# Down product waiting tile by tile, input placed in three steps, late queries inside the last unit

## The reference

```
h = layernorm(x) * w + b
win = windows of 14 x 14 of h, padded (four per image, most of them part full)
q, k, v = split(win @ qkv_w + qkv_b)                 # 12 heads of 16
a = softmax(q * scale @ k.T + rel_h(q) + rel_w(q))   # relative position terms, made from q
x1 = x + unwindow(a @ v) @ proj_w + proj_b
x  = x1 + gelu(layernorm(x1) @ up_w + up_b) @ down_w + down_b     # hidden width 768
```

## Time and profile before

| | |
|---|---|
| median of 3 runs | 676.68 us (676.61 to 677.33) |
| the profiled execution's own time | 682.86 us |
| its span, first to last instruction | 681.1 us |
| TensorE busy | 623.2 us, 92% |
| VectorE, ScalarE busy | 53%, 49% |
| GpSimd busy | 19% |

### The profile page before, as it was taken

The page is one execution under the profiler, slowest core; times in us unless marked ns, Lnnn a source line. Parts: engine busy times, 40 slices in busy tenths (PEclk is TensorE's granted clock), DMA queues, the critical chain, the costliest instruction groups (busy, mean ns, idle before and its releaser), DMA issues.

```text
span 681.1 us, 14753 instructions
## 1 busy us (share of the span) xinstructions
PE 623.2 (92%) x5696; PEld 480.5 (71%) x5696; DVE 360.6 (53%) x989; ACT 334.0 (49%) x807; POOL 129.9 (19%) x172
## 2 busy tenths in 40 slices
PE   3799999999999999999999999999999999899996
PEld 2587776777677768775877587758775876477674
DVE  4447463746374637462655365546552764426665
ACT  3326743674367435744474447543744365315453
POOL 1800032003300330023002400140013000412220
PEclk9959999999999999999999999999999999799998
DMA  4774670067205720571047003700280000000000
GB/s 110 163 154 119 135 168 7 3 133 153 69 2 124 160 59 3 113 157 36 3 87 162 22 2 77 172 22 2 66 184 21 3 3 1 1 24 1 24 24 23
DMA packets 33175, 47.51 MB, mean 70 GB/s; under 512 B 5563, under 2 KB 14331, under 8 KB 33107
## 3 DMA queue, kind: packets, MB, share of 16 engines
q1 hardware_dynamic: 31874, 46.18, 29.5%
q10 hardware_dynamic: 1232, 0.40, 0.2%
HBM read 7.25 MB, written 1.57 MB: 13 GB/s over the span
## 4 chain that ended last, share of the span: by engine, by line
issue 55%; PE 25%; POOL 12%; DVE 4%; ACT 2%; DMA 1%; POOLq 0%; ACTq 0%; SPq 0%; DVEq 0%
POOL xn L821 4%; POOL q_nat L802 3%; PE bank L631 2%; PE bank L580 2%; PE bank L625 2%; PE bank L497 2%; PE bank L516 2%; PE bank L390 2%; PE bank L431 2%; POOL x_all L808 2%; POOL x_all L814 2%; POOL rstd L795 1%; PE bank L467 1%; PE bank L614 1%; PE bank L598 1%
## 5 line engine op out<-in xcount | busy, mean ns | idle before, releaser
L1268 ACT ACTIVATE PT<-bank 98x392 f32<-98x392 f32 (+1 forms) x288 | 136.8, 490 | 134.1 <-PE bank L497 130.0
L983 DVE TENSOR_REDUCE neg_max<-bank 98x2 f32<-98x392 f32 x192 | 106.4, 562 | 116.6 <-PE bank L467 116.1
L497 PE MATMUL bank<-q_aug,k_aug 127*98 127x196 f32 (+1 forms) x672 | 112.9, 264 | 0.9 <-ACT PT L1268 0.3
L467 PE MATMUL bank<-k_aug,q_aug 126*98 126x196 f32 x384 | 87.4, 314 | 11.2 <-DVE neg_max L983 9.6
L497 PEld LDWEIGHTS bank<-q_aug,k_aug 127*98 127x98 f32 (+1 forms) x672 | 88.0, 168 | 10.5 <-ACT PT L1268 5.8
L802 POOL TENSOR_TENSOR q_nat<-st_q 96x392 f32<-96x392 f32 (+2 forms) x48 | 24.9, 546 | 330.9 <-DVE st_q L951 330.9
L580 PE MATMUL bank<-w_down,PT 128*128 128x192 f32 x384 | 74.1, 330 | 7.0 <-ACT PT L1299 7.0
L467 PEld LDWEIGHTS bank<-k_aug,q_aug 126*98 126x98 f32 x384 | 56.1, 169 | 33.7 <-DVE neg_max L983 15.9
L390 PE MATMUL bank<-xT,w_qkv 97*96 97x256 f32 (+2 forms) x272 | 75.5, 393 | 1.8 <-ACT xT L1205 1.4
L580 PEld LDWEIGHTS bank<-w_down,PT 128*128 128x128 f32 x384 | 61.8, 190 | 8.7 <-ACT PT L1299 8.2
L981 DVE TENSOR_REDUCE neg_max<-bank 120x1 f32<-120x318 f32 x96 | 46.5, 485 | 33.5 <-PE bank L463 33.4
(11 more groups left out here) (97 smaller groups left out, 968.0 us busy)
## 6 DMA issues: line engine op xcount, KB each, us to landing
q_aug<-st_q SPq DMA_DIRECT2D x64, 192.0 KB
k_aug<-st_k SPq DMA_DIRECT2D x64, 192.0 KB, 5.0
q_aug<-st_r SPq DMA_DIRECT2D x64, 168.0 KB
x_all<-in_x SPq DMA_DIRECT2D x4, 384.0 KB, 5.9
q_aug<-negT ACTq DMA_DIRECT2D x96, 1.5 KB
k_aug<-st_p SPq DMA_DIRECT2D x16, 74.2 KB, 2.3
w_up<-in_w_up SPq DMA_DIRECT2D x2, 576.0 KB, 5.0
w_down<-in_down_w SPq DMA_DIRECT2D x4, 288.0 KB, 5.6
```

Source lines behind the costliest of these rows:

```text
L467: last = t_.matmul(b[0:HALF, WIN * r:WIN * r + WIN], q_aug[0:NEG, h, c + HALF * r:c + HALF * r + HALF], k_aug[0:NEG, h, c:c + WIN], start= ...
L497: last = t_.matmul(b[0:keys, m * k:m * k + m], k_aug[0:NEG + 1, h, c + keys * k:c + keys * k + keys], q_aug[0:NEG + 1, h, c:c + m], start= ...
L983: ins = v.tensor_reduce(neg_max[0:HALF, slot(n, u), e:e + 5:4], b[0:HALF, 0:2 * WIN] .rearrange("p (r m) -> p r m", r=2), AX.X, ALU.max, n ...
L1268: s.activation(PT[0:rows, i % 8, 0:m], bank[2 + i % 2][0:rows, 0:m], ACT.Exp).then_inc(S["exp"], 1)
```

## The change

Three edits. In `down` the single wait for all six GELUs at t = 0, f = 0 becomes four: three GELUs at f = 0 (the third reads bank 2, which the product of t = 0 writes), four at f = 3, five at f = 4, six at f = 5; the early scores between the matmuls move from behind f = 1 and f = 4 to behind f = 3 and f = 5. `place_x` on VectorE is called three times, behind the row maxima of steps 1, 2 and 3 of unit 0, one piece each, and its semaphore rises three times a job. The four chunks of the late queries stand behind the four steps of unit 8.

```
-                   xT_dve=1, xT_act=1, q_mm=2, ...
+                   xT_dve=3, xT_act=1, q_mm=2, ...
...
-                    need(pe, ["xT_dve", "xT_act"][j], m, 1)
+                    need(pe, ["xT_dve", "xT_act"][j], m, [3, 1][j])
...
-                        need(pe, "xT_dve", n, 1)
+                        need(pe, "xT_dve", n, 3)
                         need(pe, "xT_act", n, 1)
...
             def down(n, t, f):
                 l = layer(n)
-                if t == 0 and f == 0:
-                    need(pe, "gelu", n, MC)
+                if t == 0 and f != 1 and f != 2:
+                    need(pe, "gelu", n, max(3, f + 1))
                 if t == 2 and f == 0:
                     need(pe, "out", n, 1)
...
-                            if u == 8 and e in (0, 3):
-                                queries_in(n + 1, 1, e // 3, 1)
+                            if u == 8:
+                                queries_in(n + 1, 1, e, 1)
...
-                if more:
-                    queries_in(n + 1, 1, 2, 2)
                 for k in range(3):
                     values(n, LAST, k)
...
                         down(n, t, f)
-                        if more and f in (1, 4):
+                        if more and f in (3, 5):
                             early_scores(n + 1, 4 + 2 * t + f // 4)
...
-            def place_x(n):
+            def place_x(n, k):
                 l = layer(n)
-                need(dve, "xT_mm", n, 1)
-                need(dve, "v_mm", n - 1, 3)
-                dve.wait_ge(ld_front[l], LD_FRONT)
-                for dst, src in pieces(xT[0:96, 0, 0:TOK], bank[front_bank(n, "x0")][0:96, :]):
-                    last = v.tensor_scalar(dst, src, affine[l][0:96, 0, 0:1], affine[l][0:96, 1, 0:1], ALU.mult, ALU.add)
-                last.then_inc(S["xT_dve"], 1)
+                if k == 0:
+                    need(dve, "xT_mm", n, 1)
+                    need(dve, "v_mm", n - 1, 3)
+                    dve.wait_ge(ld_front[l], LD_FRONT)
+                dst, src = pieces(xT[0:96, 0, 0:TOK], bank[front_bank(n, "x0")][0:96, :])[k]
+                v.tensor_scalar(dst, src, affine[l][0:96, 0, 0:1], affine[l][0:96, 1, 0:1], ALU.mult, ALU.add)\
+                    .then_inc(S["xT_dve"], 1)
...
-            place_x(0)
+            for k in range(3):
+                place_x(0, k)
...
                         if more:
-                            if (u, e) == (0, 1):
-                                place_x(n + 1)
+                            if u == 0 and e:
+                                place_x(n + 1, e - 1)
```

More of the change, by code:

```diff
@@ L192, in program @@
         PER = dict(stats1=1, stats2=2, aggr1=1, aggr2=2, veps1=1, veps2=2, rstd1=1, rstd2=2, xn1=1, xn2=2, xT_mm=2,
-                   xT_dve=1, xT_act=1, q_mm=2, q_hi=2, q_lo=2, q_nat=2, k_mm=2, k_hi=2, k_lo=2, r_tok=4, rt_copy=4, r_mm=4, r_hi=4, r_lo=4,
+                   xT_dve=3, xT_act=1, q_mm=2, q_hi=2, q_lo=2, q_nat=2, k_mm=2, k_hi=2, k_lo=2, r_tok=4, rt_copy=4, r_mm=4, r_hi=4, r_lo=4,
                    v_mm=3, v_copy=3, s_mm=HEADS, max=HEADS, nt_mm=UNITS, negT=UNITS, st_mm=HEADS, exp=HEADS,
```

## The result

The changed kernel takes 672.3 us in the median of 17 runs, the kernel before 676.8 us on the same chip. The ratio is 0.9932, 95% interval 0.9906 to 0.9958: faster by 4.5 us, or 0.7%. The forecast was 671.2 us with a range of 668.5 to 674.3.

The account below looks back on a forecast made before the run. TensorE, busy 92% of the span, was taken as the bound, so only closing its idle time pays. Terms -8.3 + 0.3 + 0.6 + 1.9 = -5.5 us took the median from 676.7 to 671.2 us, range 668.5 to 674.3.

Parts of the forecast that it names:

- down product: Down matmuls no longer wait for GELUs 5 and 6: 1.19 us saved, seven times, 8.3 us.
- last job's wait: In the last job, TensorE's 0.88 us wait around VectorE's clearing of the fold tiles grows by 0.3 us, once.
- placing: Wait before score 16 is split, not closed; first query projection still needs piece three: +0.08 us, seven times, +0.6 us.
- late queries: Last unit: two chunks moved before score 35 delay the last value product 0.27 us, seven times, +1.9 us.
- refill: TensorE array emptied at each added down wait: taken as nothing, upper bound 0.1 us each, 2.1 us in all.
- alternation on VectorE: Pieces and row maxima taking turns: might lose four overlaps, projection 0.28 us later, +2.0 us over seven jobs.
- upper end: Placing term's upper bound, +2.6 us, if VectorE instructions lose their overlap, as the skill's DRAIN rule would have it.
- (a): Rival: spread placing removes the whole 1.13 us VectorE wait before score 16; 662.7 us, chance 0.08.
- (b): Rival: late queries in the last unit cost nothing, their shift staying under 0.48 us; 669.3 us, chance 0.12.
- (c): Rival: refill at down waits or VectorE overlap lost, 2.0 to 2.1 us each; 673.3, both 675.3 us; chance 0.10.
- (d): Rival: all upper ends together, -0.1 us, no change that can be told; chance 0.04.
- (e): Rival: DMA of negated maxima into q_aug holds the next job's first transposed score, gain lost; 679.5 us, chance 0.04.

Follow-up runs that it names:

- e7: Late queries edit alone on the kernel before, with ScalarE's output copy of unit 7 put ahead of the last exponential: +0.08 us a job, one run.
- e8: Kernel before with only late query chunk 1 moved, behind step 1 of unit 8: -0.02 us a job, one run.
- e3: Late queries edit alone on the kernel before: +0.40 us a job, ratio 1.0036.
- e2: Placing in three steps alone on the kernel before: +0.10 us a job, ratio 0.9989.
- e13: Kernel before plus down edit, VectorE's pieces all in unit 1, ScalarE's in unit 0, early query chunks all in unit 2: -1.31 us a job, ratio 0.9820.
- e1: Down product's waits and moved early scores alone on the kernel before: -1.21 us a job, ratio 0.9883.
- e12: Kernel before plus down edit, VectorE's pieces two and three in unit 1, ScalarE's three in unit 0, early query chunks later: -1.49 us a job, ratio 0.9833.
- e9: Kernel before plus down edit, pieces two and three of both VectorE and ScalarE in unit 1, early query chunks later: -0.72 us a job, ratio 0.9890.
- e11: Kernel before plus down edit, all three pieces of both engines in unit 1, early query chunks in unit 2: -0.81 us a job, ratio 0.9908.

## Why the prediction was right

The time came out 1.1 us above the forecast and within its own narrower range; the terms, by one-part kernels, seven jobs each, and the last job's by its score 14:

| term | taken | measured |
|---|---|---|
| down product | -8.3 | -1.21 x 7 = -8.5 |
| last job's wait | +0.3 | +0.3 |
| placing | +0.6 | +0.10 x 7 = +0.7 |
| late queries | +1.9 | +0.40 x 7 = +2.8 |
| sum | -5.5 | -4.7 |

**Down product: right.** No refill and no gap at any of the added waits, and 1.19 us forecast against 1.21. The Trainium skill ("TensorE: Matmul & The Clock Gate", Step-by-step: what each phase is for) has weight loads pulled ahead of matmuls in flight, and leaves open whether that lasts across a wait. This trace shows that it does where the semaphore is already there: the eight instructions take the 1.18 us from 104.64 to score 4 at 105.82, and the weight load of f = 3, which waits for the fourth GELU, starts at 105.47, while the matmul in front of it (105.47 to 105.79) is at work.

**The last job: right in size, a little off in form.** The wait of 0.88 us didn't grow (0.87 after); a wait of 0.19 us for an earlier row maximum stands in front of it, and score 14 comes 0.3 us later than a job's gain alone would put it.

**Placing: right.** The wait was split, not closed: score 16 sooner by 0.50 us, the projection later by 0.06, when 0.08 had been taken. The alternation on VectorE kept its overlap: the piece that ends at 117.07 is followed at 117.00. The Trainium skill ("VectorE: DVE Perf Modes", The DRAIN you can't avoid) lets the next instruction wait for an empty pipe, but adds that one that isn't held starts earlier, which the prediction left out. The rows of both orders fit the addition, with an overlap of 0.07 us, so the section was no reason for the upper end. The forecast looked for the remainder as waits of L390 and L497. None is listed for these jobs: 0.13 us is idle before the projection, and transposed score 4 starts 0.48 us behind its score with the idle time hidden in the modelled end of the score.

**Late queries: the mechanism right, the size off.** This is the term that was mis-sized: +1.9 us taken, 2.8 measured. e7 and e8 confirm the mechanism (the cover of ScalarE's exponential and copy, a threshold above one chunk). The step that failed in size was "value product at 152.01 with the 0.05 us from an end on ScalarE to a start on TensorE", 0.27 us later. It came 0.40 later. Of the 0.13 missing, 0.09 is that last distance, 0.14 us where the copy comes last; the rest is the shift of ScalarE's last exponential, 0.77 to 0.79 us in e3 instead of 0.75. The 0.05 us was read at a down matmul that waits for one semaphore, and it holds for this product too when the exponential is last (e7).

**Rivals.** (a), the whole 1.13 us, is out: e2 is slower per job, not faster; even with all pieces out of the way (e13 against e1) 0.10 us a job was had. (b), free late queries, holds for one chunk (e8), not for two (e3). (c), refill or lost overlap, is out by the rows above: the median lies between the forecast and its 673.3, but the late queries put it there. (d), 676.6 us, is out by the interval, whose upper end is 674.0. (e), the DMA of the negated maxima as the new bound, is out by e1: all of the gain stayed.

The change as made left time behind: the down edit alone is 0.52 us a job better, and e12 0.80 us a job better than the kernel after.

## What to carry to other kernels

A list of waits names a releaser, not a price: look for what stands next in the queue and which of its inputs comes last, before a wait is counted as gain. Waits of 7.0 us for ScalarE were worth 8.5 us, because only that engine's last tile was late; a wait of 1.13 us a job for VectorE was worth at most 0.28 (e12 against e1), because the next consumer, then the pace of the row maxima (e12), then that of the exponentials (e13), stood right behind it. And work that fills a stretch in which another engine finishes a chain is cover, not clutter: moved ahead of the chain's first link, it delays the whole chain.

## What the runs showed of the hardware

- **The order in which two semaphores come matters.** For an instruction of TensorE that waits for two, the trace shows a separate wait instruction in front of the weight load for the one (147.05 to 147.10 in the kernel after), while the load carries the other. If the one on the separate instruction comes last, the matmul starts 0.14 us behind the releaser's end (the copy, in the kernel after, and ScalarE's piece in e9, too), otherwise 0.05 us (the exponential, in e7). It isn't the kind of work waited for: in e13 the exponential has the separate instruction at transposed score 4, and it starts 0.14 us behind its end (116.62 to 116.76); at transposed scores 5 and 6 the load carries it, and it is 0.05 us. That swapping the two in the program would give back the 0.09 us wasn't tried.
- **The granted clock differs from run to run on a single core**, and the time with it: single runs of the kernel after lie between 670.0 us (mean clock 0.998) and 677.3 us (0.982). In the traces the clock is 1.00 from 115 to 460 us in all, and the dips lie in front and behind: from 34 to 51 us the mean is 0.54 before, 0.90 after and 0.61 in e11 (which stays down until 68 us, 0.70), from 580 to 600 us it is 0.83 before and 1.00 after. The first dip begins in or right behind a lull: from 31 to 34 us TensorE was busy for 1.40 of 3 us before and 1.95 after. A change of 0.1 us a job can be seen only between start times within the undisturbed middle.
